# First cross-attention of a six-part block: probabilities turned on VectorE in 32x32 blocks, context weighed in four 32-key row tiles, PSUM banks shared in time

## The reference, cut to what matters

```python
h, dh = (16, 64)
q = (x @ Wq).reshape(B, Nq, h, dh)          # x: layernormed, 32 queries per sequence
k = (context @ Wk).reshape(B, Nk, h, dh)    # context: 257 keys of 96
v = (context @ Wv).reshape(B, Nk, h, dh)
scores = jnp.einsum('bqhd,bkhd->bhqk', q, k) * scale
attn = jax.nn.softmax(scores, axis=-1)
out = jnp.einsum('bhqk,bkhd->bqhd', attn, v).reshape(B, Nq, h * dh)
return out @ Wo + bo
...
x = x + _L0_xattn_ref(_layernorm(x, axis=-1), ctx_768, L0_xattn_Wq, ...)
```

## Time and profile before

| what | value |
|---|---|
| median of 3 runs | 2655.43 us (2645.6 to 2662.11) |
| span of the profiled execution | 2656.2 us |
| first unit's scores to the last statistics of this stage | 32.15 to 761.0 us |
| PE busy in the span | 94% |
| TensorE clock granted in this stage from 60 us on | 1.00 of full speed |

### The profile page before, as it was taken

How to read it: one execution, slowest core, us unless ns; L and a number is a source line. 1 busy time by engine, 2 the same in 40 slices (tenths; PEclk the granted TensorE clock), 3 DMA queues, 4 the chain that set the end, 5 groups by cost and what they waited for, 6 DMA issues and landing times. The chain is left out here.

```text
span 2656.2 us, 92968 instructions
## 1 busy us (share of the span) xinstructions
PE 2489.7 (94%) x38497; PEld 2102.8 (79%) x38497; DVE 1610.9 (61%) x3115; ACT 1418.9 (53%) x3840; POOL 1052.4 (40%) x1152
## 2 busy tenths in 40 slices
PE   6999999999989999997769998999999979899999
PEld 5888888888877888885559897677777768888888
DVE  3555555555568677674655554677777757644553
ACT  3555555555556676764644444677777734422222
POOL 1333333333341000002344444566666633345555
PEclk9999999999999999998869998999999999799999
DMA  5422222222225111110020000210101010065573
GB/s 171 154 88 88 87 88 88 87 89 87 83 93 202 40 39 47 39 47 2 1 71 1 0 0 7 60 30 24 30 24 30 19 52 0 2 134 114 107 136 75
DMA packets 60446, 168.35 MB, mean 63 GB/s; under 512 B 6685, under 2 KB 20641, under 8 KB 55465
## 3 DMA queue, kind: packets, MB, share of 16 engines
q1 hardware_dynamic: 60330, 166.71, 21.3%
HBM read 145.18 MB, written 21.51 MB: 63 GB/s over the span
## 5 line engine op out<-in xcount | busy, mean ns | idle before, releaser
L566 POOL TENSOR_TENSOR l_probs<-l_probs,l_rden 128x1024 f32<-128x1024 f32 x128 | 242.2, 1892 | 434.8 <-DVE l_rden L424 434.8
L508 ACT ACTIVATE l_probs<-ps,l_nmax 128x257 f32<-128x257 f32 x512 | 236.0, 474 | 228.3 <-DVE l_nmax L418 228.3
L967 POOL TENSOR_TENSOR l_probs<-l_probs,l_rden 128x1024 f32<-128x1024 f32 x128 | 242.3, 1893 | 175.9 <-DVE l_rden L818 175.9
L418 DVE TENSOR_REDUCE l_nmax<-ps 128x2 f32<-128x514 f32 x256 | 165.5, 688 | 222.1 <-PE ps L303 222.1
L903 ACT ACTIVATE l_probs<-ps,l_nmax 128x257 f32<-128x257 f32 x512 | 236.0, 474 | 59.9 <-DVE l_nmax L812 59.9
L2722 POOL TENSOR_TENSOR m_hh<-m_hh,m_cb 128x512 f32<-128x512 f32 (+1 forms) x136 | 179.6, 1321 | 142.2 <-DVE m_hh L2674 134.5
L303 PE MATMUL ps<-l_ctxQ,l_q 32*128 32x257 f32 x3072 | 204.5, 395 | 7.1 <-ACT l_probs L508 6.4
L812 DVE TENSOR_REDUCE l_nmax<-ps 128x2 f32<-128x514 f32 x256 | 165.5, 688 | 62.2 <-PE ps L704 58.8
L2578 ACT ACTIVATE m_sg<-ps 128x512 f32<-128x512 f32 (+1 forms) x136 | 81.3, 598 | 220.4 <-PE ps L138 219.5
L823 DVE COPY l_pT<-ps 128x512 f32<-128x512 f32 x256 | 165.0, 686 | 53.6 <-PE ps L713 49.4
L2674 DVE TENSOR_TENSOR m_hh<-ps,m_sg 128x512 f32<-128x512 f32 (+1 forms) x136 | 94.0, 691 | 168.8 <-PE ps L138 152.9
(11 more groups left out here) (371 smaller groups left out, 6485.8 us busy)
## 6 DMA issues: line engine op xcount, KB each, us to landing
l_ctxQ<-in_ctx_q SPq DMA_DIRECT2D x32, 1542.0 KB, 6.5
enc_dash<-kept SPq DMA_DIRECT2D x32, 512.0 KB, 3.3
m_cb<-combined SPq DMA_DIRECT2D x32, 512.0 KB, 10.6
l_ctxT<-in_ctx_t SPq DMA_DIRECT2D x32, 385.5 KB, 3.3
l_ctxK<-in_ctx_k SPq DMA_DIRECT2D x32, 384.0 KB, 3.1
m_cb<-combined SPq DMA_DIRECT2D x16, 768.0 KB, 15.5
kept<-enc_va SPq DMA_DIRECT2D x10, 512.0 KB, 3.3
m_cb<-combined SPq DMA_DIRECT2D x16, 256.0 KB, 4.6
```

What stands on the lines that cost most here:

```text
L418: nc.vector.tensor_reduce(nmax[:, par, 2 * half:2 * half + 2], ps[:, S_B + 2 * half:S_B + 2 * half + 2, 0:NK], AX.X, ALU.max, negate=True) ...
L508: nc.scalar.activation(probs[:, par, hg, :], ps[:, S_B + hg, 0:NK], ACT.Exp, bias=nmax[:, par, hg:hg + 1], accum_out=den[:, par, hg:hg + 1 ...
L566: nc.gpsimd.tensor_tensor(pr, pr, rden[:, b, :, None].to_broadcast([P, HG, NK - 1]), ALU.mult).then_inc(norm_ok, 1)
L967: nc.gpsimd.tensor_tensor(pr, pr, rden[:, b, :, None].to_broadcast([P, HG, K_W]), ALU.mult).then_inc(norm_ok, 1)
```

## The change

- PE no longer turns the probabilities. POOL writes the normalised ones to a new buffer `pn` (two units deep), DVE turns it by one instruction of 128x1024 (each 32x32 block in place) into `pT`. The copies L461 and L537 are gone.
- Since the blocks are 32x32, keys lie on 32 partitions of each head group: `weigh_ctx` contracts 32 keys at a time, 8 blocks x 4 head groups = 32 matmuls (64 instructions). The four groups lie on four row tiles and write banks 4 to 7 (`W_B`); the stationary operand is 32x96 of the context, the moving one 32x128 of `pT`. `ctxK` is stored four times over the partitions: 1536 KB per tile.
- The result has 96 rows in four banks. DVE copies three banks at once (`moved`, 96x384), ACT the fourth in three copies of 32x128 onto partitions 96 to 127. `sum_heads` stays at 12 matmuls that contract 128 rows; only the order of the rows in `oT` and `U2` is another.
- Banks are shared in time: queries go to bank 0 (`Q_B` = `S_B`), after the first exponential of unit u+1 has read it; the next scores wait for the copy of them. `sum_heads` goes to bank 4 (`Y_B` = `W_B`), after `moved`; the next weighing waits for the add to x. It runs in three parts at b = 1, 2, 3 (3, 3 and 6 matmuls plus the last), each closed by its own add to x. The transpose of x goes to bank 5 at b = 3.
- The bias comes in with key 256's matmul (a row of ones in `last_p`, the bias in a row of `last_w`), so L93 is gone. Normalising the x of the tile after next moves from b = 2 to the end of b = 0 on DVE, behind inverse(u+1).
- At the start: queries 0 to 2 alternate between two banks; `make_chunks` has 24 matmuls instead of 48; W shares its space with `oT`, so the first turning waits for the transfer to DRAM; the second `ctxK` shares its space with early weights and is loaded after `make_chunks`.

```diff
@@ PE
+            def weigh_ctx(v, b, j):
+                pe.wait_ge(pt_ok, v + 1)
+                pe.wait_ge(oa_sb, v + 1)
+                pe.wait_ge(ov_sb, v + 1)
+                pe.nop(nofuse=True)
+                for m in range(NB):
+                    for h in range(HG):
+                        r = N * h
+                        last_i = nc.tensor.matmul(ps[0:C, W_B + h, 0:P], ctxK[j][r:r + N, b, m, :], pT[r:r + N, b % 2, :, m, :],
+                                                  start=m == 0, stop=m == NB - 1)
+                last_i.then_inc(o_mm, 1)
...
                     if b < SEQ - 1:
+                        if not last:
+                            pe.wait_ge(q_sb, NQ * t + NQ + b)
                         pe.wait_ge(exp_ok, 4 * u + 4)
                         scores(b + 1, j)
                     elif not last:
-                        pe.wait_ge(q_sb, NQ * t + 2 * NQ - 1)
+                        pe.wait_ge(q_sb, NQ * t + 2 * NQ)
                         pe.wait_ge(ctx_in[1 - j], 32 * fills)
                         pe.wait_ge(exp_ok, 4 * u + 4)
-                        scores(0, 1 - j, last_chunk=NQ * t + 2 * NQ)
...
+                        if b == (1 if first else 0) and not last:
+                            pe.wait_ge(xt_sb, t + 2)
+                        if not first:
+                            pe.wait_ge(x_ok, 3 * t - 2 + max(b - 1, 0))
                         weigh_ctx(u - 1, (b - 1) % SEQ, j if b else 1 - j)
-                    turn_probs(t, b, has_query)
-                    if b < NQ and not first:
-                        sum_heads(b, 1 - j, t - 1)
+                    if b < NQ and not last:
...
+                        pe.wait_ge(exp_ok, 4 * u + 5)
+                        queries(b)
+                    if b > 0 and not first:
+                        pe.wait_ge(oa_sb, 4 * t + 1)
+                        pe.wait_ge(ov_sb, u + 1)
+                        sum_heads(t - 1, 1 - j, parts[b], b == SEQ - 1)
+                    if b == SEQ - 1 and x_after:
+                        pe.wait_ge(ov_sb, u + 1)
+                        turn_x(t + 2)
@@ DVE
+            def turn_probs(u, b):
+                dve.wait_ge(norm_ok, u + 1)
+                nc.vector.transpose(pT[:, b % 2, :, :, :].rearrange("p g m n -> p (g m n)"),
+                                    pn[:, b % 2, :, :].rearrange("p g n -> p (g n)")).then_inc(pt_ok, 1)
...
+                        moved(u - 1, (b - 1) % SEQ, j if b else 1 - j)
+                    turn_probs(u, b)
+                    if has_s:
                         inverse(u + 1, (b + 1) % SEQ)
-                    if b == NQ - 1 and not first:
-                        residual(t - 1)
+                    if b > 0 and not first:
+                        residual(3 * t - 4 + b, t - 1)
+                        if b == SEQ - 1:
+                            count(3 * t - 1, t - 1)
+                    if b == 0 and x_after:
+                        normalise(nc, k, xn[:, :], t + 2).then_inc(xn_ok, 1)
+                    if b == SEQ - 1 and x_after:
+                        turned(t + 2)
@@ ACT
                     if b < SEQ - 1 or not last:
-                        exps(u + 1, (b + 1) % SEQ)
+                        exps(u + 1, (b + 1) % SEQ, again=not start_unit)
...
-                    act.wait_ge(t_mm, 2 * u + 1)
-                    nc.scalar.copy(pT[:, 0, :], ps[:, T_B, :]).then_inc(pt_a, 1)
+                    if b < NQ and not last:
+                        queries(NQ * t + NQ + b, 1 - j, b)
+                    if not start_unit:
+                        moved(u - 1, (b - 1) % SEQ, j if b else 1 - j)
```

More of the change, by code:

```diff
@@ L86, in clear_sems @@
         self.sems = []
-def add_to_x_and_count(nc, k, chain, t, psum, bias, xs=None):
-    xt = at(k.x, t)
-    chain.done(nc.vector.tensor_tensor(xt, psum, xt, ALU.add))
-    chain.done(nc.vector.tensor_tensor(xt, xt, bias, ALU.add))
-    nc.vector.nop(nofuse=True)
-    return nc.vector.bn_stats(at(k.stats, t), xt)
 def rstd_dve(nc, k, dve, ln, eps):
@@ L317, in sum_heads @@
+            def sum_heads(t, j, items, end):
+                for i in items:
+                    n, g = i // HG, i % HG
+                    last_i = nc.tensor.matmul(ps[:, Y_B, 0:D], oT[j][:, n, g, :, :].rearrange("p b n -> p (b n)"),
+                                              U2[:, n, g, :], start=i == items[0], stop=not end and i == items[-1])
+                if end:
+                    pe.wait_ge(lw_in, 16 * (HG * SEQ + 1))
                     pe.wait_ge(last_ok, t + 1)
                     pe.nop(nofuse=True)
-                    nc.tensor.matmul(ps[:, A_B, 0:D], last_bd[:, j, :, :].rearrange("p b n -> p (b n)"),
-                                     at(last_w, t), start=False, stop=True).then_inc(out_mm, 1)
@@ L351, in tile @@
                     start_unit = first and b == 0
-                    has_query = not last and b > 0
-                    has_x = not last and b == 0
-                    if has_query:
-                        pe.wait_ge(pt_v, u)
-                        queries(b - 1)
-                    if has_x:
-                        if not first:
-                            pe.wait_ge(o_sb, u)
-                        turn_x(t + 1)
                     if b < SEQ - 1:
+                        if not last:
+                            pe.wait_ge(q_sb, NQ * t + NQ + b)
                         pe.wait_ge(exp_ok, 4 * u + 4)
@@ L397, in _ @@
             make_last()
-            pe.wait_ge(wv_sb, 2)
             tiles(pe, tile)
+            pe.wait_ge(x_ok, 3 * T - 2)
             weigh_ctx(4 * T - 1, SEQ - 1, (T - 1) % 2)
-            for n in range(NQ):
-                sum_heads(n, (T - 1) % 2, T - 1)
+            pe.wait_ge(oa_sb, 4 * T + 1)
+            pe.wait_ge(ov_sb, 4 * T + 1)
+            sum_heads(T - 1, (T - 1) % 2, range(NQ * HG), True)
         @block.vector
@@ L440, in tile, with count @@
+            def count(n, t):
+                dve.wait_ge(x_ok, n + 2)
+                nc.vector.nop(nofuse=True)
+                nc.vector.bn_stats(at(k.stats, t), at(k.x, t))
             def tile(t, j, fills, first=False, x_after=True, last=False):
-                chain.tile(0 if first else 2 * t - 2)
                 for b in range(SEQ):
                     u = 4 * t + b
-                    if b == 0 and not last:
-                        turned(t + 1)
-                    if b < SEQ - 1 or not last:
-                        maxima(u + 1, (b + 1) % SEQ)
-                    if b == 2 and x_after:
-                        normalise(nc, k, xn[:, :], t + 2).then_inc(xn_ok, 1)
-                    if not (first and b == 0):
-                        moved(u - 1, (b - 1) % SEQ, j if b else 1 - j)
+                    has_s = b < SEQ - 1 or not last
@@ L462, in tile @@
-                    if b < SEQ - 1 or not last:
-                        inverse(u + 1, (b + 1) % SEQ)
-                    if b == NQ - 1 and not first:
-                        residual(t - 1)
+                        nc.vector.tensor_copy(U2[:, 1, :, :], ps[:, W_B + 1, :].rearrange("p (g d) -> p g d", g=HG)
+                                              ).then_inc(u2v_sb, 1)
+                        turned(1)
+                        dve.wait_ge(w_out, 16)
+                    else:
+                        moved(u - 1, (b - 1) % SEQ, j if b else 1 - j)
@@ L484, in _ @@
             normalise(nc, k, xn[:, :], 0).then_inc(xn_ok, 1)
-            chain = Chain(dve, steps, 1)
             turned(0)
@@ L577, in tile @@
                 for b in range(SEQ):
-                    normal(4 * t + b, b, j)
+                    normal(4 * t + b, b, j, again=not first or b > 1)
                     if b == 0 and not first:
```

265 lines of the change are left out of this document (121 added, 144 removed).

## The result

The changed kernel takes 2633.15 us (median of 7 executions, 2629.75 to 2640.21) against 2655.43 (also 7 executions, not 3, 2645.6 to 2662.11). The medians differ by 22 us. The ratio, worked out from the single executions and not the quotient of the medians (0.9916), is 0.9925, interval 0.9906 to 0.9943: 15 to 25 us less, 20 in the middle. The prediction had 2614, that is 42 us less. The direction holds, but about half of the gain is not there: 2633 lies outside the 2598 to 2628 of the forecast itself, and in the whole range only because that takes in the first rival (2629 to 2657). The profiled execution has a span of 2630.4 us.

The account below looks back on a forecast made before the run. PE was taken to set the pace, with the loop over the score banks next. Inner tiles 1.17 us times 30 (35.1) plus 7.2 at the start made 42.3 off: 2613, said as 2614; range 2598 to 2655, the forecast's own 2598 to 2628.

Parts of the forecast that it names:

- the first rival: Small losses stay: 0.21 us a unit from scores to weighing, or normalising caught by POOL; 2629 to 2657 us, chance 0.27.
- the signs that the prediction named for being wrong: The wait before the scores names the exponentials or DVE, or a tile's time is not within 20.6 to 21.9 us.
- PE to ACT's copy: Units b = 0 to 2: next scores wait for ACT's copy of the queries, 5.03 us a unit; b = 3 takes 5.85.
- Scores to weighing: On PE in each unit: no loss between these matmul groups, weighing starts 1.30 us after the scores instead of 1.51.
- The signal: End of ACT's query copy to the next scores at b = 0 to 2: 0.05 us, from +4.98 to +5.03.
- the 0.1 held for normalising: Allowance per tile on DVE: normalising caught by POOL's multiplication would cost 0.7 us, otherwise nothing; 0.1 was taken.
- DMA: Context loads in the tile loop: 1542 KB in 6.5 us, asked for some 15 us ahead, so covered; share about 0.37.
- The start: Before tile 1: first scores at 30.1, then 37.8, 48.3 and 62.8 instead of 70.02; gain 7.2 us, 3 either side.
- The tail: The last tile, without queries: changes by parts under 1 us each way, so nothing gained or lost.
- DVE, ACT, normalising: In each unit: DVE's turning takes 1.25 us, covered up to 2.4; ACT's three copies covered; normalising 0.34 unless caught.
- The second rival: Weight loads bound the weighing: 3.0 us a unit, 2763 or 2813 us; decides from 2.15; chance 0.12 with the third rival.
- the third rival: PE's 0.75 us idle at b = 0 lowers the clock; each tenth up to 2 us a tile; 0.12 with the second rival.

Follow-up runs that it names:

- run 7: The changed kernel with the wait for the query copy placed last ahead of the scores: 2622.33 us, ratio 0.9879 to the kernel before.
- run 2: The changed kernel loading only a quarter of the context values' columns for tiles 2 to 29: 2631.59 us, ratio 0.9903 to the kernel before.
- run 1: The changed kernel with the next stage's weight loads issued behind the loop over tiles: 2626.39 us, ratio 0.9894 to the kernel before.
- run 3: The kernel before, with context values loaded three more times per loop tile into a buffer nobody reads: 2656.81 us, ratio 0.9991.
- even parts: The changed kernel with the twelve `sum_heads` matmuls split 4, 4, 4 instead of 3, 3, 6: 2621.33 us, ratio 0.9883 to the kernel before.
- run 9: The changed kernel with DVE turning the probabilities twice, first into a buffer nobody reads: 2650.73 us, ratio 0.9988 to the kernel before.
- runs 7 and 8: Besides run 7: the changed kernel without the scores' wait for the exponentials in three of four units, 2634.66 us, ratio 0.9917 to the kernel before.

## Why the prediction was right or wrong

Two steps of the prediction failed and make up the miss: the contexts' loads were not covered for tile 2 (with the slow clock behind it 10.1 of the 10.5 us that the stretch from tile 1 to tile 2 lacks), and the loop of a unit was forecast 0.15 us too short, in two of its terms (most of the 11.5 us that 29 tiles lack). The tail adds 1.7 and the start gives back 0.3; together these are the 23.5 us that the stage lacks, but for rounding. None of the signs that the prediction named for being wrong has come: the wait names ACT's copy, the tile (21.44) lies within 20.6 to 21.9, and tile 1 begins near 62.8. It named none for the DMA. That 2633 lies near the first rival's 2639 is in good part chance, since half of the distance is the stall, which that rival doesn't have.

- *PE to ACT's copy, right.* At b = 0 to 2 the wait before the scores names ACT's copy of the queries. The loop's steps against the forecast: scores to weighing 1.40 for 1.30, weighing to queries 1.86 for 1.88, queries to copy 1.19 for 1.21, copy 0.59 for 0.59, its end to scores 0.13 for 0.05. Sum 5.17 for 5.03. b = 3: 5.87 for 5.85.
- *Scores to weighing, mis-sized.* "I expect no loss between them: weighing starts at T+1.30" failed: 0.10 of the 0.21 stays, half of what the first rival said. No run takes this apart. The Trainium skill, page "TensorEngine Tiling (Array Packing)", section "Key Properties", has a change of tiling mode drain PE; this pair differs in columns (128 and 96) but not in rows, and loses half of what the earlier trace rows show where the rows differ too. The trace shows no full drain at this pair: the weighing's weight loads start at 315.04, 0.22 us before its first matmul (315.26), beside the last scores. In before, loads (305.50 in the earlier trace rows) and matmuls of the weighing start together:

```profile
305.50 1.52 PE L343 MATMUL ps<-l_pT,l_ctxK 128*32 128x128 f32 x48
```

- *The signal, mis-sized.* "T' = +5.03" took 0.05 from the copy to the scores; it is 0.13 in the loop and 0.05 outside (run 7). The tile: 3 x 0.15 for these two, 0.02 at b = 3, 0.05 for the unit of 5.27 in every other tile (not explained), less the 0.1 held for normalising: 0.4, the step from 21.04 to 21.44, 12 us over 29 tiles and half of the stage's error. That the signal's part can be had back is shown by run 7 (0.28 a tile).
- *DMA, wrong.* "SP issues nothing else. Covered" holds for the inner tiles (run 2) and fails for tile 2: before its contexts SP sends the next stage's weights (3.9 MB in the list of DMA issues), and the request leaves 8.0 us before it is wanted, not the forecast's "some 15". The contexts come at 85.7 and are wanted at 78.0. I had read the 6.5 us of the earlier trace rows, a median over 32 loads, and not the one load that meets the weights. Stall 7.7 and slow clock 2.4 us: 10 us, nearly the other half; run 1 gives them back.
- *The start, right with a reserve:* 31.13, 36.27, 46.28 and 62.57 against 30.1, 37.8, 48.3 and 62.8. The gain of 7.5 rests on before's 70.03; run 3 has 65.11 with the same code and "even parts" 60.17 with after's, so a pair of executions shows anything between 2.5 and 9.9, and that it came out so near to 7.2 is partly luck. What it gave, the stall took back: the earlier start reached a load that came no sooner.
- *The tail, wrong by 1.7.* "Nothing" overlooked that with the banks shared in time the weighing has to wait for the add to x, where nothing else is left to do. In the last tile it does so twice, 0.48 each; the rest of the 1.7 isn't taken apart. Timeline of after:

```profile
733.40 1.58 PE L307 MATMUL ps<-l_U,l_late 128*128 128x128 f32 x12 [0.76 <-DVE l_late L388]
...
735.67 2.00 PE L299 MATMUL ps<-l_pT,l_early 32*96 32x128 f32 x64 [0.48 <-DVE x L414]
```

- *DVE, ACT, normalising, right.* Turning 1.23 for 1.25 and covered (run 9). ACT's three copies take 0.79 together and hide. Normalising is not caught:

```profile
313.75 0.31 DVE L96 TENSOR_SCALAR l_xn<-x,mean,rstd 128x128 f32 x1
...
313.91 1.91 POOL L558 TENSOR_TENSOR l_pn<-l_probs,l_rden 128x1024 f32<-128x1024 f32 x1 [3.41 <-DVE l_rden L400]
```

- *The second rival, refuted.* 64 pairs in 1.86 us leave 0.116 a pair on each of four row tiles, and the 128 moving columns alone take 0.107. So a load of 96 columns is hidden behind a matmul of its own row group. By a rule of the Trainium skill, page "TensorE: Matmul & The Clock Gate", section "The mechanism", a load overlaps only matmuls of other row groups; the trace does not agree. (The same section also lets a load into the background weight buffer go ahead of running matmuls, which would fit.) The rival's turning point was also mis-worked: by the forecast's own sum a tile reaches 22.2 at 2.00 us of weighing, not at 2.15; at 1.86 neither is met. A lower clock, the third rival, came in one place only, after the stall (0.92 and 0.85), by an idle of 7.74 us and not by the 0.75 that the rival names; with 1.6 us of idle a tile the clock stays at 1.00.

## What to carry to other kernels

A loader that is "covered" in the steady state must be checked once more where it queues behind another stage's loads, and against the new, earlier time at which it is wanted: a faster start only moves the wait. When an engine stops being the bound, write down the loop that closes next (here scores, maxima, exponential, queries, copy) and its length; gains add only until then, and two edits that each save alone may share one slack. Ask also when the load is sent: the engine that issues it may be busy with other requests. Measure a stage by its own ends and its period: the rest of the program moved by up to 16 us between kernels that share it.

## What the runs showed of the hardware that was not expected

- The place of a wait: of two waits ahead of the scores, with the late one first, the scores start 0.13 us after the signal inside the hardware loop and 0.05 in unrolled code; with the late one last it is 0.05 in the loop, and the unrolled units are 0.09 longer (runs 7 and 8). A single wait is short in both.
- A load of 96 columns for every matmul of 128 columns on 32 rows costs nothing that shows: 0.029 us a pair over four row tiles, against 0.027 for the moving columns alone by the pace of the earlier trace rows (an estimate).
- DVE's turning of 1024 elements on 128 partitions takes 1.23 us, of 512 0.71 and of 32 0.20: 1.0 to 1.1 ns for each element added. All 128 of the stage take 1.23, beside POOL and PE at work.
- Contexts at 147 GB/s instead of 90, with the DMA engines 40% busy instead of 27%, left the tile as it was, 21.46 us (run 2), and so in before (22.21, run 3).
